# The second mixture of experts: rows weighed in their slots, added by accumulating scatters to a table of sums, the last expert writing the output

## The reference, cut to what matters

```python
z = xf @ proj_w.T + proj_b                        # 8 experts
s = jax.nn.sigmoid(z) + expert_bias               # scores; the best two weigh w1 + w2 = 1
topk_w, topk_idx = jax.lax.top_k(probs, 2)
...
kept_w, kept_pair = jax.lax.top_k(wmat, cap)      # each expert keeps its 640 heaviest tokens
xe = xf[kept_tok]
h = gelu(einsum('ecd,ehd->ech', xe, fc1_w) + fc1_b)       # 256 -> 512
oe = einsum('ech,edh->ecd', h, fc2_w) + fc2_b             # 512 -> 256
y = zeros.at[kept_tok].add(oe * kept_w)           # a token gets 0, 1 or 2 contributions
sh = gelu(xf @ sh1_w.T + sh1_b) @ sh2_w.T + sh2_b         # shared expert, every token
x = x + tanh(g_ffn[1]) * (sh + y)
```

## Time and profile before

| | |
|---|---|
| median of three runs | 1041.64 us (1035.23 to 1043.22) |
| span of the profiled execution | 1038.9 us, no other time of it is recorded |
| busy share of TensorE, VectorE, ScalarE, GpSimd | 91%, 71%, 60%, 30% |
| mean granted TensorE clock | 0.955 of full speed |
| second mixture | from about 768 us to the end |
| its experts | from 895 us to 1022 us, TensorE busy 125.09 of 127 us |
| after TensorE's last matmul | 17 us |

### The profile page before, as it was taken

One profiled execution on the slowest core, in us unless ns is written; L12 is line 12 of the kernel. 1 busy time (PEld: TensorE's weight loads), 2 busy tenths in 40 slices (PEclk: granted clock), 3 DMA queues, 4 the chain that ended last, 5 costly groups with the idle time before them and its releaser, 6 DMA issues. The chain is left out here.

```text
span 1038.9 us, 21998 instructions
## 1 busy us (share of the span) xinstructions
PE 945.9 (91%) x7942; PEld 874.9 (84%) x7942; DVE 739.1 (71%) x1810; ACT 619.0 (60%) x1500; POOL 306.9 (30%) x362
## 2 busy tenths in 40 slices
PE   5899998778897789999999999999979999899993
PEld 4688876677785579999999999999979999899992
DVE  7888887776688778776665656565676778476655
ACT  4788886476896345555555555555547444566650
POOL 3444434026004235222222222222100000566741
PEclk9899999789999889999999999999988999899997
DMA  9611210004641101000000000003033000535517
GB/s 273 198 48 58 63 63 2 2 26 124 199 127 52 36 21 42 12 21 2 22 1 21 1 22 1 22 1 103 1 110 95 1 1 1 137 133 151 148 58 268
DMA packets 64617, 69.24 MB, mean 67 GB/s; under 512 B 11488, under 2 KB 56032, under 8 KB 64384
## 3 DMA queue, kind: packets, MB, share of 16 engines
q1 hardware_dynamic: 57680, 52.22, 16.3%
q0 software_dynamic: 5712, 15.36, 5.4%
q10 hardware_dynamic: 1120, 0.27, 0.2%
HBM read 46.07 MB, written 21.76 MB: 65 GB/s over the span
## 5 line engine op out<-in xcount | busy, mean ns | idle before, releaser
L1782 POOL TENSOR_TENSOR a_probs<-a_probs,a_softmax 128x512 f32<-128x512 f32 x64 | 66.8, 1043 | 298.0 <-DVE a_softmax L1836 298.0
L1595 PE MATMUL a_psK<-a_kvThi,a_wk 128*128 128x512 f32 x256 | 97.8, 423 | 3.6 <-DVE a_klo L1821 3.6
L1846 DVE TENSOR_TENSOR a_ulo<-a_psU,a_uhi 128x512 fp32r<-128x512 f32 x64 | 44.2, 691 | 66.9 <-ACT a_uhi L1732 66.9
L314 POOL TENSOR_SCALAR t_neg<-t_raw,t_nthr 128x256 bf16<-128x256 f32 (+1 forms) x54 | 60.6, 1138 | 104.3 <-DVE t_nthr L543 98.3
L1720 ACT ACTIVATE a_probs<-a_psS,a_softmax 128x256 f32<-128x256 f32 x128 | 59.6, 470 | 37.6 <-DVE a_softmax L1831 37.6
L2369 POOL DMA_INDIRECT rows<-m_tokens,r_comes x40 | 40.3, 1008 | 124.0 <-DVE r_comes L2579 111.9
L1635 PE MATMUL a_psU<-a_pThi,a_tokhi 128*128 128x256 f32 x256 | 72.8, 284 | 2.3 <-DVE a_pTlo L1841 2.3
L1654 PE MATMUL a_psY<-a_nwhi,a_uhi 128*128 128x256 f32 x256 | 73.4, 287 | 1.2 <-DVE a_ulo L1846 1.2
L1710 ACT ACTIVATE a_khi<-a_psK,a_bk 128x512 fp32r<-128x512 f32 x64 | 44.1, 689 | 48.0 <-PE a_psK L1595 47.7
L1635 PE MATMUL a_psU<-a_pTlo,a_tokhi 128*128 128x256 f32 x256 | 72.4, 283 | 0.0
L1635 PE MATMUL a_psU<-a_pThi,a_toklo 128*128 128x256 f32 x256 | 72.4, 283 | 0.0
(11 more groups left out here) (412 smaller groups left out, 3182.6 us busy)
## 6 DMA issues: line engine op xcount, KB each, us to landing
t_raw<-in_L_ffn_expert_w SPq DMA_DIRECT2D x16, 512.0 KB, 3.6
f_raw<-in_fc_T SPq DMA_DIRECT2D x16, 512.0 KB, 3.9
m_results<-a_zeros SPq DMA_DIRECT2D x8, 512.0 KB, 3.5
m_sorted<-m_zeros SPq DMA_DIRECT2D x1, 2944.0 KB, 12.6
m_n<-m_sorted SPq DMA_DIRECT2D x23, 128.0 KB, 2.9
m_expert_out<-e_y SPq DMA_DIRECT2D x23, 128.0 KB, 1.7
a_rawkv<-in_L_xattn_Wkv SPq DMA_DIRECT2D x8, 256.0 KB, 6.4
m_n<-in_sh_T SPq DMA_DIRECT2D x2, 1024.0 KB, 8.4
```

The costliest lines, as they stand in the source:

```text
L314: ins = pool.tensor_scalar(neg[:, own], raw[h % NRAW][:, own], nthr[h % 2][:, n:n + 1], None, ALU.is_lt)
L1595: ins = pe.matmul(psK[:].rearrange("p b t -> p (b t)"), wk[x][:, a, h * DH:(h + 1) * DH], kvT[pair % 2][y][:, a, :, :, :].rearrange("p b m ...
L1782: pool.tensor_tensor(own, own, rsum[:, n % NM, :].unsqueeze(2).to_broadcast([P, 2, 2 * P]), ALU.mult).then_inc(s["p_done"], 1)
L1846: dve.tensor_tensor(u[ch % 2][1][:], psU[ch % 2][:], u[ch % 2][0][:].bitcast(F32), ALU.subtract).then_inc(s["u_lo"], 1)
```

## The change

- **Table of sums.** `yg`, its eight zeroing DMAs and the tile of zeros are gone. A DRAM table `acc` of 2048 rows (and 640 behind them for empty slots) takes its place. After each pair's `keep` SyncE writes the pair's two blocks of `x_sb` to it (8 DMAs of 256 KB, and one of 640 KB for the rows behind). The shared bias is now added to `x_sb` by GpSimd, before `keep`, early in the first stage; `keep` waits for it.
- **Weights travel with the rows.** A row of the token table `xr` becomes 264 floats: 256 and the token's eight weights, zero where an expert didn't keep it, times the gate. VectorE makes them in one instruction in the "room" step; SyncE writes them by a DMA of 2048 pieces of 32 bytes. The gather brings row and weights together. There are three sets of 5 gather buffers instead of two, so the eleventh gather waits for nothing.
- **Put.** VectorE multiplies the expert's bias by the slot's weight (`b2w`) ahead of the wait for `xdown`, and then takes the PSUM tile times the weight plus `b2w`, into one of eight buffers.
- **Send.** The scatter of experts 0 to 6 adds to `acc` (`compute_op=ALU.add`). The five tiles of one expert have distinct tokens, but two experts can share a token, so ahead of an expert's first scatter GpSimd waits until all scatters before it have landed (`landed`); ahead of the very first, until `acc` is written.
- **Last expert.** When the scatters of the first seven have landed, SyncE copies `acc` to the output, DRAM to DRAM, in four DMAs of 512 KB, and at the same time GpSimd fetches the last expert's rows of `acc` by five gathers (`fetch`). For its tiles 0 and 1 VectorE adds the fetched sums after the put (`join`), for tiles 2 to 4 within `b2w`. When the copy has landed, GpSimd scatters the five tiles straight to the output (`finish`); empty slots are out of bounds and skipped. The last loads, the 32 weighing additions and the write of `x_sb` are gone.
- **Order.** In LATE the fourth down-step of the expert before the last stands ahead of the third up-step of the last. The router's `order` steps are gone, since it doesn't matter any more which of a token's two experts comes first, and `index_all` has one instruction less.

```diff
-                for n in range(2):
-                    load_results(n)
-                for j in range(GROUPS):
-                    own = slice(j * PG, (j + 1) * PG)
-                    sp.wait_ge(s["combined"], NB + (j + 1) * PG)
-                    sp.dma_start(out[own].rearrange("b p d -> p b d"), x_sb[:, own, :]).then_inc(s["out_done"], 16)
+                for b in range(NS):
+                    sp.wait_ge(y_out[b], ((NE - 1) * NT + NS - 1 - b) // NS * 16)
+                own = NTOK // COPIES
+                for i in range(COPIES):
+                    sp.dma_start(out_rows[i * own:(i + 1) * own], acc[i * own:(i + 1) * own]).then_inc(s["copied"], 16)
...
+                for i in range(PAIRS):
+                    own = slice(2 * i, 2 * i + 2)
+                    sp.wait_ge(s["kept"], 2 * i + 2)
+                    sp.dma_start(acc_b[:, own, :], x_sb[:, own, :]).then_inc(s["acc_in"], 16)
+                    if i == (NT - 1) // 2:
+                        sp.dma_start(acc[NTOK:NTOK + CAP].rearrange("(t p) d -> p t d", p=P), x_sb[:, 0:NT, :]).then_inc(s["acc_in"], 16)
+                    if i == WEIGHED:
+                        sp.wait_ge(s["weighed"], 1)
+                            sp.dma_start(xr_b[:, :, D:DW], weight[:]).then_inc(s["rows_out"], 16)
                 sp.wait_ge(s["turned"], NT)
...
                 def send(e, t):
                     n = e * NT + t
+                    if t == 0 and e == 0:
+                        pool.wait_ge(s["acc_in"], (PAIRS + 1) * 16)
+                    elif t == 0:
+                        landed(n)
                     pool.wait_ge(s["y_done"], n + 1)
-                    pool.indirect_dma_start(yg, bass.IndirectOffsetOnAxis(ap=goes[:, n:n + 1], axis=0), y[n % NY][:], None)\
-                        .then_inc(y_out[n % NY], 16)
+                    pool.indirect_dma_start(acc, bass.IndirectOffsetOnAxis(ap=goes[:, n:n + 1], axis=0), ys[n % NS], None,
+                                            compute_op=ALU.add).then_inc(y_out[n % NS], 16)
+                def fetch(t):
+                    n = (NE - 1) * NT + t
+                    if t == 0:
+                        landed(n)
+                    pool.indirect_dma_start(sums[t], None, acc, bass.IndirectOffsetOnAxis(ap=comes[:, n:n + 1], axis=0)).then_inc(sums_in[t], 16)
+                def finish(t):
+                    n = (NE - 1) * NT + t
+                    if t == 0:
+                        pool.wait_ge(s["copied"], COPIES * 16)
+                    pool.wait_ge(s["y_done"], n + 1)
+                    if t < HELD:
+                        pool.wait_ge(s["joined"], t + 1)
+                    pool.indirect_dma_start(out_rows, bass.IndirectOffsetOnAxis(ap=goes[:, n:n + 1], axis=0), ys[n % NS], None,
+                                            bounds_check=NTOK - 1, oob_is_err=False).then_inc(s["out_done"], 16)
...
                 def put(e, t):
                     n = e * NT + t
+                    own = xin[e % NX][:, t, D + e:D + e + 1]
+                    dve.wait_ge(x_in[e % NX][t], e // NX * 16 + 16)
+                    if e == NE - 1 and t >= HELD:
+                        dve.wait_ge(sums_in[t], 16)
+                        dve.scalar_tensor_tensor(out=b2w[n % 2], in0=xb2[:, e, :], scalar=own, in1=sums[t], op0=ALU.mult, op1=ALU.add)\
+                           .then_inc(s["b2_done"], 1)
+                    else:
+                        dve.tensor_scalar(b2w[n % 2], xb2[:, e, :], own, None, ALU.mult).then_inc(s["b2_done"], 1)
                     dve.wait_ge(s["xdown"], n + 1)
-                    at_least(dve, y_out[n % NY], n // NY * 16)
-                    dve.tensor_tensor(y[n % NY][:], psY[n % 2][:, 0, :], xb2[:, e, :], ALU.add).then_inc(s["y_done"], 1)
+                    at_least(dve, y_out[n % NS], n // NS * 16)
+                    dve.scalar_tensor_tensor(out=ys[n % NS], in0=psY[n % 2][:, 0, :], scalar=own, in1=b2w[n % 2],
+                                             op0=ALU.mult, op1=ALU.add).then_inc(s["y_done"], 1)
-        LATE = [("d", 0), ("u", 0), ("d", 1), ("u", 1), ("d", 2), ("d", 3), ("u", 2), ("d", 4), ("u", 3), ("u", 4), ("u", 5),
+        LATE = [("d", 0), ("u", 0), ("d", 1), ("u", 1), ("d", 2), ("d", 3), ("d", 4), ("u", 2), ("u", 3), ("u", 4), ("u", 5),
                 ("next d", 0), ("u", 6), ("u", 7), ("next d", 1)]
```

More of the change, by code:

```diff
@@ L2016, in feed_forward_1 @@
         assert SETS * (P + 3 * TILES) <= space.shape[1]
+        NS = 2 * NY
+        ys = [t[:] for t in y] + [listing[:, n, :] for n in range(NY)]
+        b2w = [listing[:, NY + n, :] for n in range(2)]
+        sums = [listing[:, NY + 2 + t, :] for t in range(NT)]
         count_i, count_b = sb("r1_count_i", [P, P], I32, c), sb("r1_count_b", [P, P], BF16, c)
@@ L2136, in _ @@
                     sp.dma_start(xb2[:], A["L1_ffn_fc2_b"].partition_broadcast(P)).then_inc(s["b_in"], 16)
+                for i in range(PAIRS):
[6 more added lines that the diff above has]
+                        sp.wait_ge(s["weighed"], 1)
+                        with nc.allow_non_contiguous_dma(reason="eight weights behind each row"):
+                            sp.dma_start(xr_b[:, :, D:DW], weight[:]).then_inc(s["rows_out"], 16)
                 sp.wait_ge(s["turned"], NT)
@@ L2378, in _, with landed, bias @@
+                def landed(n):
+                    for b in range(NS):
+                        at_least(pool, y_out[b], (n + NS - 1 - b) // NS * 16)
+                def bias(i):
+                    if i >= LAST:
+                        pool.wait_ge(s["row_done"], i - LAST + 1)
+                    pool.tensor_tensor(x_sb[:, i, :], x_sb[:, i, :], b2s[:], ALU.add).then_inc(s["x_biased"], 1)
                 pool.iota(iota_i[:], pattern=[[1, NE]], base=0, channel_multiplier=0).then_inc(s["iota_done"], 1)
@@ L2387, in _ @@
                 ins.then_inc(s["bits_done"], 1)
-                pool.wait_ge(s["rows_out"], 32)
+                for i in range(NB):
+                    bias(i)
+                pool.wait_ge(s["rows_out"], 48)
                 pool.wait_ge(s["n_turned"], NB)
@@ L2393, in _ @@
                         gather(e, t)
-                for e in range(NE):
+                for e in range(NE - 1):
                     for t in range(NT):
@@ L2398, in _ @@
                             gather(e + 3, t)
-                for b in range(NY):
-                    pool.wait_ge(y_out[b], (NE * NT + NY - 1 - b) // NY * 16)
+                for t in range(NT):
+                    fetch(t)
+                for t in range(NT):
+                    finish(t)
+                pool.wait_ge(s["out_done"], NT * 16)
             @block.vector
@@ L2412, in keep @@
                     n = 2 * i + j
+                    dve.wait_ge(s["x_biased"], n + 1)
                     dve.wait_ge(s["down"], n + 1)
```

134 lines of the change are left out of this document (45 added, 89 removed).

## The result

The changed kernel took 1067.36 us (median of four runs, 1063.98 to 1073.24) beside 1040.22 for the kernel before: a ratio of 1.028 with a 95% interval of 1.0244 to 1.0317 (the two medians alone divide to 1.026). It is slower, where I had forecast 1034 and a range up to 1045.

The account below looks back on a forecast made before the run. TensorE was taken to bound the kernel (91% busy) until 1022 us, leaving a 17 us end to win. End -8.3 and passage +0.7 sum to -7.6 us, 1034 us; range 1026 to 1045.

Parts of the forecast that it names:

- Bias additions on GpSimd: Early in the second mixture's first stage: 16 x 0.74 = 11.8 us, costing nothing under GpSimd's 111.88 us of idle time.
- Ten issues at 1.29 are 12.9 us: GpSimd's queue per expert: five scatters and five gathers fit in a period of 15.35 us.
- L: Landing time of an expert's last accumulating scatter, taken as 4.0 us; GpSimd's cycle 10.3 + L stops fitting at 5.05.
- rival C: In the experts, GpSimd's queue becomes the bound through late landings or a longer accumulating issue: 1045 to 1065 us, chance 0.12.
- the other door: In the experts, GpSimd's queue also becomes the bound if the accumulating issue holds GpSimd 1 us longer.
- The fetches ... land by 1021.9 (4.0 us) or 1024.7 (6.8 us): At the end, five fetches issued from 1012.7 every 1.3 us stay hidden if the copy lands later than about 1019.
- 8.9 + 0.7: The 2 MB copy at the end: 8.9 us like a load beside other traffic, plus 0.7 for the five fetches.
- End: 1022.3 + 8.3: Copy done at 1022.3, then five finishing scatters issued and landed in 8.3 us: end at 1030.6.
- -8.3: The predicted gain at the kernel's end: 1030.6 against 1038.9 us.
- A lag hurts only when it reaches the end: In the experts, gathers three experts ahead and eight y buffers (24 us) cover any lag of GpSimd's queue before the end.
- signs of being wrong: Scatters landing over 5 us with growing waits; fifth-transpose idle changed over 2 us; last put awaiting a fetch; finishing scatters awaiting y.
- The passage (+0.7): From shared expert to experts: writes of sums and 1056-byte rows beside the gathers cost 0.7 us, bounds -4.4 to +3.

Follow-up runs that it names:

- experiment 1: The changed kernel with the 16 shared-bias additions made by VectorE just ahead of each keep, none by GpSimd: 1059.72 us, ratio 1.0182 to the kernel before.
- Experiments 5 to 8: Kernel before with accumulating scatters (1.009), these plus the landing wait (1.0151), the wait with plain scatters (0.9981); last, experiment 1 with plain scatters (1.0053).
- 8: The changed kernel with bias additions on VectorE and the scatters of experts 0 to 6 writing instead of adding: ratio 1.0053 to the kernel before.
- experiment 9: The changed kernel with bias additions on VectorE, plain scatters, and the copy to the output cut to 16 rows: ratio 0.998 to the kernel before.
- 10: The changed kernel with each of the copy's four DMAs moving 4 rows instead of 512: ratio 1.0224 to the kernel before.
- experiment 5: The kernel before with its 40 scatters adding to the zeroed table of results, no wait added: ratio 1.009, median 1048.0 us, profiled execution 1039.77 us.

## Why the prediction was wrong, step by step

**1. "Bias additions on GpSimd: ... GpSimd idled 111.88 us."** Mis-stepped. The cover was read from GpSimd's own idle time; I asked who would wait for GpSimd and not whom GpSimd would stop. Price: 9.2 us in the span, 1.0% between the changed kernel and experiment 1, 0.6% for the same stop in the kernel before. The row that I quoted, a gather waiting for `r_comes` from VectorE, says that this stretch belongs to VectorE. The Trainium skill, "SBUF — State Buffer", section "SBUF: two separate sides", says that VectorE and GpSimd share one pair of ports under an exclusive lock, held for a whole instruction of whichever starts first (of VectorE's instructions only some kinds take it). I hadn't drawn on it. The trace agrees that the two exclude each other, and differs in how long: one instruction of VectorE waited for fourteen or sixteen of GpSimd in a row.

**2. "Ten issues at 1.29 are 12.9 us."** The step that cost most. The accumulation's landing was bounded from both sides, and its issue was taken over from the plain scatter without a bound. At 1.59 us the ten issues are 15.9 us, of which 3.2 cover the landing: 12.7 + L, with L = 3.9 an estimated 16.6 against a period of 15.35. On the chip it is 18.4: from an expert's last scatter to the next one's first it takes 4.1 to 5.0 us, not 3.9, and some issues were longer too (the first scatter up to 2.27 us, gathers up to 1.73). That is rival C, the queue as the bound, by the door that it names itself (an issue that holds GpSimd longer); its time came out just above its range of 1045 to 1065, which is luck in part, since only the experts' 12.4 us and the later end are C's; the additions, the fetches and the drain are not in it. I gave it 0.12, because I looked for a landing three times as long, and the other door had no price. Experiments 5 to 8: issue alone 1.009, with the wait 1.0151, wait alone 0.9981, and experiment 1 better by 1.3% with the plain scatter.

**3. "The fetches ... land by 1021.9 (4.0 us) or 1024.7 (6.8 us)."** Mis-sized by the same habit. I charged the copy 0.7 us for the fetches and the fetches nothing for the copy. Both together move 2.6 MB; the fetches take 10.5 us, as 8, 9 and 10 show (4.6 to 4.8 without the copy). I asked only whether the last put would wait for the fifth fetch. The third put waits for the third, issued at 1040.95 and awaited until 1051.28; with it waits the addition for tile 0 behind it, and TensorE for its last down-step. So the fetches and not the copy set the first finishing scatter: 1053.86, where the copy, with its last piece issued at 1039.5 and landing in at most 10.8, was done by 1050.3. The copy itself took between 10.8 us, the landing of its slowest piece, and 12.7 us from first issue, against my 8.9 + 0.7 and inside my bounds (6.9 to 13.9). The Trainium skill's formula ("DMA: Bandwidth & Descriptors", section "Anatomy of one DMA"), by which I had estimated 6.8 us for it, falls short of this; the section gives it for DMAs that GpSimd issues, and this copy is SyncE's.

**4. "End: 1022.3 + 8.3."** The scatters were right: 7.5 us from the first to the landing of the last. Missing is the drain of 5.5 us, which the trace of before shows at 1025.2 and which I had not read. From the landing of the seventh expert's scatters to the end I had 17.9 us; it was 29.7. Of the 11.8 more, 6.4 are the fetches (1053.86 against 1037.6 + 9.6 + 0.3) and 5.9 the drain with the instructions behind it, less 0.5 of quicker scatters. That landing itself comes 4.0 us later against TensorE's last down-steps, which fits GpSimd's lag from point 2. Together they turn -8.3 into the +7.6 of the ledger.

**What held.** The accumulation lands in 3.9 us (4.0). The writes of the sums (2.1 to 2.7 us each), the pieces of 32 bytes (2.9) and VectorE's extra work in the experts cost little to be seen (the experts are 1.5 us longer in 8 and 9, of which 0.7 is the wait named at the end of this paragraph); the wait for the landing is free by itself (0.9981). "A lag hurts only when it reaches the end" did not hold: TensorE waited for gathers behind the scatters in the same queue long before the end. The reordering of down-steps has a price that I left out: the last expert's second weights come later, and TensorE waits 1.33 us ahead of its first down-step at 1032.40, 0.67 before. Of the prediction's own signs of being wrong two came, a put that waits for a fetch and finishing scatters that wait for y; scatters landing in over 5 us in the median did not. The passage (+0.7) can't be judged: -2.2 in the ledger is less than what executions differ by.

Of the forecast's sum, -7.6, the runs leave -2 at best (experiment 9, whose interval includes no change). Its end is 3.3 us shorter in the trace and its experts 1.5 longer: most of the gain was spent on the five scatters and the drain that took the old chain's place. What stays open is why the stage ahead of the experts differs by up to 6 us between executions of kernels that run the same work in it (110.5 to 116.9).

## What to carry to other kernels

An engine's idle time is cover for itself only: before work moves there, ask which engines it can stop, and read what was critical in that stretch. A DMA with another operation has two prices, how long its issue holds the queue and how long it takes to land; bound both. Where the end of a program is rebuilt, the last instruction's own tail (a drain hidden until now) and the transfers that will run side by side belong into the sum. And compare executions stage by stage: the span of experiment 5 showed nothing of what its stages show.

## What the runs showed of the hardware

- An accumulating indirect scatter of 128 rows of 1 KB holds GpSimd 1.59 us (plain 0.99) and lands in 3.9 to 4.1 us (plain 2.8 to 3.1), by the medians of the five kernels with it and of the others whose trace has them.
- A 128x2 instruction of VectorE took 10.0 to 10.1 us beside fourteen additions of GpSimd and 4.45 beside sixteen memsets.
- GpSimd's drain at the program's end took 4.67, 5.48, 6.59 or 6.99 us, the same number wherever it stood in kernels with the same kinds of indirect transfers (5.48 in the changed kernel and in experiments 1 and 10), so it seems to go with what was issued and not with when.
- Gathers from DRAM beside a 2 MB copy within DRAM landed in 10.5 to 11.0 us, without it in 4.6 to 4.8.
